# Layer norm and hi/lo split of x: the low half made by a matmul in PSUM, the norms moved to GpSimd and VectorE

## The reference, cut to what matters

```python
x = L0_attn_x                                  # (16, 512, 128) float32
xn = _layernorm(x, axis=-1)                    # (x - mean) / sqrt(var + 1e-5)
s = _L0_attn_ref(xn, ...)                      # token shift, r/k/v projections, recurrence by chunks, output projection
g = _silu(_L0_ffn_ref(xn, ...))                # gate logits = xn @ gate_W.T, top 2 of 8 experts, 8 shared experts
x = x + s * g
```

## Time and profile before

| | |
|---|---|
| median of 3 runs | 736.77 us (736.12 to 741.37) |
| the profiled execution | 736.52 us, span of its trace 734.7 us |
| busy | PE 657.6 us, DVE 575.1 us, ACT 484.7 us, POOL 454.7 us |
| granted TensorE clock, mean | 0.985 |
| `dve_choose(0)` starts | 47.51 us after the span's start |

### The profile page before, as it was taken

One profiled execution on the slowest core, in us unless ns is written; L12 is line 12 of the kernel. 1 busy time (PEld: TensorE's weight loads), 2 busy tenths in 40 slices (PEclk: granted clock), 3 DMA queues, 4 the chain that ended last, 5 costly groups with the idle time before them and its releaser, 6 DMA issues.

```text
span 734.7 us, 22308 instructions
## 1 busy us (share of the span) xinstructions
PE 657.6 (90%) x8520; PEld 457.7 (62%) x8520; DVE 575.1 (78%) x1095; ACT 484.7 (66%) x985; POOL 454.7 (62%) x490
## 2 busy tenths in 40 slices
PE   2677787997999999999999999999997899999993
PEld 1444465665666665566666667788895667666672
DVE  6989997987677886667676667666764899999996
ACT  5865578684666666566666666666665677877772
POOL 2434322225777777777777777677777566666763
PEclk9999999998999999999999999999999999999997
DMA  9931112101111232433323334323444757767642
GB/s 243 278 101 44 44 44 86 60 3 35 45 45 51 95 102 90 151 109 105 105 95 109 104 105 151 99 96 106 105 109 119 216 197 230 230 200 212 209 138 58
DMA packets 88616, 86.75 MB, mean 118 GB/s; under 512 B 11394, under 2 KB 65284, under 8 KB 88516
## 3 DMA queue, kind: packets, MB, share of 16 engines
q1 hardware_dynamic: 79428, 66.70, 29.1%
q0 software_dynamic: 9088, 18.63, 9.7%
HBM read 50.82 MB, written 34.47 MB: 116 GB/s over the span
## 4 chain that ended last, share of the span: by engine, by line
PE 43%; DVE 30%; issue 9%; POOL 8%; ACT 6%; DMA 3%; SPq 0%; DVEq 0%; ACTq 0%; POOLq 0%
PE banks L1509 7%; PE banks L1510 7%; PE banks L1511 7%; DVE wwords L1259 7%; DVE hidden L1276 6%; DVE hidden L1174 5%; PE banks L1549 5%; POOL expert_rows L629 4%; PE banks L1529 4%; PE banks L1530 4%; PE banks L1528 4%; POOL srows L619 3%; ACT hidden L747 2%; ACT hidden L743 2%; DMA srows<-normed_rows,source 2%
## 5 line engine op out<-in xcount | busy, mean ns | idle before, releaser
L747 ACT CAST hidden<-hidden 128x512 f16<-128x512 f32 x206 | 127.2, 618 | 144.1 <-DVE hidden L1174 144.0
L1178 DVE TENSOR_TENSOR hidden<-hidden 128x512 f16<-128x512 f32 x178 | 122.9, 691 | 82.4 <-ACT hidden L747 81.4
L619 POOL DMA_INDIRECT srows<-normed_rows,source x142 | 148.8, 1048 | 54.0 <-issue 40.5
L1174 DVE TENSOR_TENSOR hidden<-hidden,banks 128x512 f32<-128x512 f32 x206 | 140.7, 683 | 42.4 <-ACT hidden L743 37.1
L1528 PE MATMUL banks<-wwords,hidden 128*128 (+1 forms) x824 | 149.8, 220 | 1.4 <-DVE hidden L1178 1.0
L1530 PE MATMUL banks<-wwords,hidden 128*128 (+1 forms) x824 | 149.7, 220 | 0.0
L1529 PE MATMUL banks<-wwords,hidden 128*128 (+1 forms) x824 | 149.7, 220 | 0.0
L743 ACT ACTIVATE hidden<-banks 128x512 f32<-128x512 f32 x206 | 122.8, 596 | 27.9 <-PE banks L1511 27.7
L1509 PE MATMUL banks<-sx,wwords 128*128 128x512 f16 (+1 forms) x368 | 121.5, 330 | 0.6 <-DVE sx L1167 0.6
L1511 PE MATMUL banks<-sx,wwords 128*128 128x512 f16 (+1 forms) x368 | 121.6, 330 | 0.0
L1510 PE MATMUL banks<-sx,wwords 128*128 128x512 f16 (+1 forms) x368 | 121.5, 330 | 0.0
(11 more groups left out here) (213 smaller groups left out, 1416.0 us busy)
## 6 DMA issues: line engine op xcount, KB each, us to landing
rows<-x SPq DMA_DIRECT2D x32, 256.0 KB, 5.2
rows<-expert_rows SPq DMA_DIRECT2D x32, 256.0 KB, 3.4
normed_rows<-rows SPq DMA_DIRECT2D x16, 256.0 KB, 3.9
r_rows<-rows SPq DMA_DIRECT2D x16, 256.0 KB, 2.1
rd_rows<-rows SPq DMA_DIRECT2D x16, 256.0 KB, 2.0
stage<-r_rows SPq DMA_DIRECT2D x16, 256.0 KB, 5.4
k_rows<-rows SPq DMA_DIRECT2D x16, 256.0 KB, 2.1
kd_rows<-rows SPq DMA_DIRECT2D x16, 256.0 KB, 2.1
```

What stands on the lines that cost most here:

```text
L619: G.indirect_dma_start(srows[:, q % NXB, t, :], None, rows_in, bass.IndirectOffsetOnAxis(source[:, at:at + 1], 0)).then_inc(sem[f"s_in{q % ...
L747: A.copy(guh[:, i % 4, :], gu[:, i % 2, :]).then_inc(sem["gu_hi"], 1)
L1174: V.tensor_tensor(gu[:, i % 2, :], sg[:, i % 2, :], psum[2 * (i % 2) + 1][:, :], ALU.mult).then_inc(sem["gated"], 1)
```

## The change

- The low half: `pe_rest` adds to the transposed batch, still in its bank, the product of a negative identity and `xh` (one 128x512 float16 matmul). What is left in the bank is x minus its high half. ScalarE copies it to `xl` (`act_rest`). VectorE's `dve_flip` is gone. `minus_one` is made once by ScalarE. The transposes set the bank's start flag only with the first of four.
- The norms: ScalarE norms nothing more. VectorE norms tile 0 (`OWN_NORMS` is 1), GpSimd tiles 1 to 3, as `(row - mean) * rstd`; `shift` is gone, and the norms wait for `rstd`.
- `rates * gap` is computed by GpSimd (`pool_gaps`), ahead of its first norm.
- Order: VectorE does `dve_stats(0)` ahead of everything else. The weights' split and `dve_r_weights` follow the loop on VectorE; ScalarE's parts of the split move to its rounds 14 to 16. ScalarE copies a batch three rounds after its `std` and its rest four rounds after. On TensorE `pe_up(0)` stands behind `pe_rest(15)`.

```diff
+            def pool_gaps():
+                G.wait_ge(sem["const_in"], 16)
+                G.wait_ge(sem["rates"], 4)
+                G.tensor_tensor(wtmp[:, :, :], rep(rates[:, :], Q), rep_mid(C("gap"), HEADS), ALU.mult).then_inc(sem["gaps"], 1)
+
             def pool_norm(b):
-                G.wait_ge(sem["shift"], b + 1)
-                for t in range(b * TPS + TPS // 2, (b + 1) * TPS):
-                    G.tensor_scalar(rows[:, t, :], rows[:, t, :], rstd[:, t:t + 1], shift[:, t:t + 1],
-                                         ALU.mult, ALU.add).then_inc(sem["normed_g"], 1)
+                G.wait_ge(sem["rstd"], b + 1)
+                for t in range(b * TPS + OWN_NORMS, (b + 1) * TPS):
+                    G.tensor_scalar(rows[:, t, :], rows[:, t, :], mv[:, t, 0:1], rstd[:, t:t + 1],
+                                    ALU.subtract, ALU.mult).then_inc(sem["normed_g"], 1)
...
-            def act_norm(b):
-                A.wait_ge(sem["shift"], b + 1)
-                for t in range(b * TPS, b * TPS + TPS // 2):
-                    A.activation(rows[:, t, :], rows[:, t, :], ACT.Identity, bias=shift[:, t:t + 1],
-                                      scale=rstd[:, t:t + 1]).then_inc(sem["normed_a"], 1)
-
...
+            def act_rest(b):
+                A.wait_ge(sem["x_rest"], b + 1)
+                A.copy(xl[:, b * XS + 2:(b + 1) * XS], psum[b % 4][:, :]).then_inc(sem["x_lo"], 1)
...
-            for b in range(nb + 3):
+            for b in range(nb + 4):
                 if b < nb:
                     act_std(b)
-                if 1 <= b <= nb:
-                    act_norm(b - 1)
-                if 2 <= b < nb + 2:
-                    act_flip(b - 2)
-                if 10 <= b < 13:
-                    act_split_w(0, b - 10)
+                if 3 <= b < nb + 3:
+                    act_flip(b - 3)
+                if b >= 4:
+                    act_rest(b - 4)
+                if FIRST_SPLIT <= b < FIRST_SPLIT + 3:
+                    act_split_w(0, b - FIRST_SPLIT)
...
-                V.scalar_tensor_tensor(shift[:, T4], mv[:, T4, 0], -1.0, rstd[:, T4], ALU.mult, ALU.mult).then_inc(sem["shift"], 1)
-
-            def dve_flip(b):
-                V.wait_ge(sem["x_hi"], b + 1)
-                V.tensor_tensor(xl[:, b * XS + 2:(b + 1) * XS], psum[b % 4][:, :], xh[:, b * XS + 2:(b + 1) * XS],
-                                     ALU.subtract).then_inc(sem["x_lo"], 1)
+                for t in range(b * TPS, b * TPS + OWN_NORMS):
+                    V.tensor_scalar(rows[:, t, :], rows[:, t, :], mv[:, t, 0:1], rstd[:, t:t + 1],
+                                    ALU.subtract, ALU.mult).then_inc(sem["normed_v"], 1)
...
+            dve_stats(0)
             dve_prologue()
             dve_rates()
-            for b in range(nb + 3):
+            for b in range(1, nb + 1):
                 if b < nb:
                     dve_stats(b)
-                if 1 <= b <= nb:
-                    dve_norm(b - 1)
-                if b >= 3:
-                    dve_flip(b - 3)
-                if 11 <= b < 14:
-                    dve_split_w(0, b - 11)
-                if b >= nb + 1:
-                    dve_r_weights(b - nb - 1)
+                dve_norm(b - 1)
+            for part in range(3):
+                dve_split_w(0, part)
+            dve_r_weights(0)
+            dve_r_weights(1)
...
+            def pe_rest(b):
+                if b == 0:
+                    T.wait_ge(sem["minus_one"], 1)
+                T.wait_ge(sem["x_hi"], b + 1)
+                T.matmul(psum[b % 4][:, :], minus_one[:, :], xh[:, b * XS + 2:(b + 1) * XS], start=False, stop=True,
+                         skip_group_check=True).then_inc(sem["x_rest"], 1)
...
-            for b in range(nb + 3):
-                if 2 <= b < nb + 2:
-                    pe_flip(b - 2)
-                if b == nb + 1:
+            for b in range(nb + 2):
+                if b < nb:
+                    pe_flip(b)
+                if 1 <= b <= nb:
+                    pe_rest(b - 1)
+                if b == nb:
                     pe_up(0)
-                if b >= 3:
-                    pe_gate(b - 3)
+                if b >= 2:
+                    pe_gate(b - 2)
```

More of the change, by code:

```diff
@@ L144, in build @@
         rstd = take([P, NT])
-        shift = take([P, NT])
         gate32 = sb("gate32", [P, EXPERTS])
@@ L238, in build @@
         f2y = sb("f2y", [P, P], F16)
+        minus_one = f2
         take = carve(rows[:, :, :].rearrange("p a b -> p (a b)"))
@@ L391, in lows @@
             return sum(low_on_pool(j) == on_pool for j in range(i + 1))
+        OWN_NORMS = 1
+        FIRST_SPLIT = 14
         LOWS_FIRST = 12
@@ L463, in sp_normed @@
             def sp_normed(b):
-                nc.sync.wait_ge(sem["normed_a"], (b + 1) * TPS // 2)
-                nc.sync.wait_ge(sem["normed_g"], (b + 1) * TPS // 2)
+                nc.sync.wait_ge(sem["normed_v"], (b + 1) * OWN_NORMS)
+                nc.sync.wait_ge(sem["normed_g"], (b + 1) * (TPS - OWN_NORMS))
                 nc.sync.dma_start(rows_in[b * SEQ:(b + 1) * SEQ, :].rearrange("(t p) d -> p t d", p=P),
@@ L676, in pool_program @@
             pool_prologue()
+            pool_gaps()
             for b in range(nb):
@@ L718, in act_flip, with act_minus_one @@
                 A.copy(xh[:, b * XS + 2:(b + 1) * XS], psum[b % 4][:, :]).then_inc(sem["x_hi"], 1)
+            def act_rest(b):
+                A.wait_ge(sem["x_rest"], b + 1)
+                A.copy(xl[:, b * XS + 2:(b + 1) * XS], psum[b % 4][:, :]).then_inc(sem["x_lo"], 1)
+            def act_minus_one():
+                A.wait_ge(sem["const_in"], 16)
+                A.mul(minus_one[:, :], C("ident"), -1.0).then_inc(sem["minus_one"], 1)
             def act_split_w(k, part):
@@ L791, in act_decays @@
             def act_decays():
-                A.wait_ge(sem["const_in"], 16)
-                A.wait_ge(sem["rates"], 6)
+                A.wait_ge(sem["rates"], 5)
+                A.wait_ge(sem["gaps"], 1)
                 A.activation(wmat[:, :, :], wtmp[:, :, :], ACT.Exp, scale=-1.0).then_inc(sem["decays"], 1)
@@ L841, in act_program @@
             act_rates()
+            act_minus_one()
             act_decays()
-            for b in range(nb + 3):
+            for b in range(nb + 4):
                 if b < nb:
                     act_std(b)
-                if 1 <= b <= nb:
-                    act_norm(b - 1)
-                if 2 <= b < nb + 2:
-                    act_flip(b - 2)
-                if 10 <= b < 13:
-                    act_split_w(0, b - 10)
+                if 3 <= b < nb + 3:
[4 more added lines that the diff above has]
+                    act_split_w(0, b - FIRST_SPLIT)
             for i in range(NS + LAG):
@@ L917, in dve_rates @@
                 V.tensor_scalar(rates[:, :], rates[:, :], 200.0, None, ALU.min).then_inc(sem["rates"], 1)
-                V.wait_ge(sem["rates"], 4)
-                V.tensor_tensor(wtmp[:, :, :], rep(rates[:, :], Q), rep_mid(C("gap"), HEADS), ALU.mult).then_inc(sem["rates"], 1)
+                V.wait_ge(sem["rates"], 3)
                 V.tensor_scalar(nrate[:, :], rate[:, :], -1.0, None, ALU.mult).then_inc(sem["rates"], 1)
@@ L1419, in pe_flip @@
                     T.wait_ge(sem["const_in"], 16)
-                T.wait_ge(sem["normed_a"], (b + 1) * TPS // 2)
-                T.wait_ge(sem["normed_g"], (b + 1) * TPS // 2)
+                T.wait_ge(sem["normed_v"], (b + 1) * OWN_NORMS)
+                T.wait_ge(sem["normed_g"], (b + 1) * (TPS - OWN_NORMS))
                 for t in range(TPS):
-                    i = T.transpose(psum[b % 4][:, t * P:(t + 1) * P], rows[:, b * TPS + t, :], C("ident"))
+                    i = T.matmul(psum[b % 4][:, t * P:(t + 1) * P], rows[:, b * TPS + t, :], C("ident"), start=(t == 0), stop=(t == TPS - 1),
+                                 is_transpose=True)
                 i.then_inc(sem["flipped"], 1)
+            def pe_rest(b):
[4 more added lines that the diff above has]
+                         skip_group_check=True).then_inc(sem["x_rest"], 1)
             def pe_gate(b):
```

## The result

The changed kernel takes 749.6 us (median of 4 runs, 747.4 to 756.09) against 738.17 us for the kernel before beside it (4 runs): ratio 1.0172, interval 1.0131 to 1.0213. Run again on another occasion it took 745.68 (6 runs) against 737.66 (11 runs): 1.0125, 1.0098 to 1.0153. It is slower by 8 to 11 us; I had forecast 3.8 us faster. The profiled execution took 747.4 us, its span 745.2. The table has times in us, from that execution's trace and from the one before.

What follows compares the result with a forecast made beforehand. VectorE's own work was taken to set the prologue's pace; rounds of 1.57 us, GpSimd's norms ending at 38.2 and a 5.5 us chain put dve_choose(0) at 43.7, 3.8 sooner: 733.0 us, range 730.2 to 737.2.

Steps and rivals of the forecast that it cites:

- The head: Prologue's start: dve_stats(0) free in the wait for constants; gap product 2.3 us on GpSimd, first reciprocal at 11.8, 1.0 later.
- The round: Each prologue round falls from 2.05 to 1.57 us; the other engines hold it, GpSimd's three norms taking 1.31.
- my own list of signs: What would show the forecast right or wrong, such as GpSimd's norms above 0.45 or pe_up(0)'s matmuls 0.22 apart.
- VectorE's round: VectorE in the prologue: 2.05 less 0.60 subtraction and 0.08 shift, plus 0.20 for one norm, 1.57 us.
- The tail: Prologue's end: three splits stretch GpSimd's last norms by 1.5 us, to 38.2; then a 5.5 us chain to dve_choose(0).
- The sum: 38.2 + 5.5 puts dve_choose(0) at 43.7, 3.8 us sooner; the median time is 733.0 us.
- the part on later stages: After the prologue: what dve_choose(0) gains, the end gains, unless something late takes it back; later stages keep their length.
- My own range for the forecast: 731.8 to 734.8 us: cheap gap product and no tail contact take 2.6 off, dearer product and lost slack add 1.2.
- The higher clock: Rival, 25%: TensorE reaches its higher clock before the tail; pe_up(0) 1.3 us shorter, the rest 0.2, time 731.5.
- The rival on the slow side: Rival, 12%: TensorE and ScalarE waiting on each other set the prologue's pace, round 2.2 us, time 741.4.

Runs made afterwards that it cites:

- experiment 1: The changed kernel with GpSimd's three norms as row * rstd + shift again, shift computed by VectorE: 732.14 us against 737.14 for the kernel before, ratio 0.9938.
- experiment 2: The changed kernel with GpSimd's three tiles as (subtract mean, multiply by rstd), (multiply by rstd, add mean), (add mean, multiply by rstd); no kernel time given.
- experiment 6: The changed kernel with GpSimd's norms as (row + negated mean) * rstd, VectorE negating the means: 732.42 us against 736.75 for the kernel before, ratio 0.9924.
- experiment 10: The version of experiment 9 with ScalarE's copy of a batch two rounds after its std instead of three: 742.49 us against 736.16, ratio 1.0086.
- experiment 8: The version of experiment 7 with VectorE's three weight splits behind GpSimd's last norm and dve_r_weights ahead of them: 728.77 us against 736.75, ratio 0.9877.
- experiment 7: The version of experiment 6 with the product of rates and gaps back on VectorE: 732.22 us against 736.75 for the kernel before, ratio 0.9932.
- experiment 5: The changed kernel with two norms of a batch on VectorE and two on GpSimd: 737.58 us against 737.14 for the kernel before, ratio 1.0006.
- experiment 3: The changed kernel with GpSimd's tiles as (multiply by rstd, subtract mean), (subtract mean) alone, (subtract a constant, multiply by rstd); no kernel time given.
- experiment 4: The kernel before with GpSimd's two norms of a batch as (row - mean) * rstd: 738.68 us against 737.14, ratio 1.0033.
- experiment 9: The version of experiment 8 with the low half on VectorE again, no rest matmul and no second copy: 746.73 us against 737.66, ratio 1.0135.

## Why the prediction was wrong, by its own steps

- **The head** was right. The gap product took 1.90 us on GpSimd (2.3 taken, 1.22 to 2.47 bounded), the first reciprocal came at 11.57 (11.8). `dve_stats(0)` was free: it ran from 3.56, before the constants.
- **The round: the failed step** is the sentence that three norms on GpSimd take 1.31, 0.43 each. They took 2.32, 0.77 each. I priced the new norm by the old row and never set the two forms side by side, though the diff shows both: (multiply, add) before, (subtract, multiply) now. The operand kinds and the shape were the same, the operation was not. Experiments 1, 2 and 6 show that this alone carries the loss: with either form without a subtraction, and all else kept but for one small operation on VectorE, `dve_choose(0)` comes 10.5 to 11.4 us sooner. I had even bounded unknown prices elsewhere, but held this one for known, although my own list of signs had "GpSimd's norms longer than 0.45 in the middle of the prologue (then it sets the pace)". Why a subtraction is slow on GpSimd stays open.
- **VectorE's round.** Where GpSimd doesn't hold it, it is 1.64, not 1.57: VectorE's norm is 345 ns long and 0.26 from start to start. The 285 ns row multiplied by one scalar per partition and by a constant, the norm has two scalars per partition and a subtraction; no run tells the two differences apart. By the Trainium skill ("VectorE: DVE Perf Modes", how the mode is chosen) the norm could handle two elements a cycle, which would have made it shorter than I took it; it came out longer, and the measurement decides.
- **The tail.** Three splits beside six norms cost 1.5 us (4.17 in experiment 1, against 2.61 in experiment 10), as forecast, and experiment 8 took 1.05 of it back. The Trainium skill, "SBUF — State Buffer" (the section on its two sides), says that a VectorE operation with two SBUF inputs and a GpSimd one that reads SBUF lock each other out for whole instructions; 0.5 us lost for each 0.65 us split fits it, though no run shows that the lock lasts for the whole instruction.
- **The sum with the price mended.** Experiment 1 is close to my forecast with its assumption made true: `dve_choose(0)` at 43.87 (43.7 forecast), 732.14 us (733.0 forecast). That the numbers meet is luck: GpSimd's last norm ended at 40.11 and not at 38.2, because of the slower round, and the chain behind it took 3.76 and not 5.5, because of the higher clock. What was gained there reached the end, as the part on later stages said.
- **The range.** My own range for the forecast, 731.8 to 734.8, is not what its terms give: 2.6 off and 1.2 on make 730.4 to 734.2.
- **The rivals.** The higher clock came true in experiments 1 and 8. It was worth 1.3 us in `pe_up(0)`, as priced, and 0.6 in the transposes and the rest, where I had 0.2. The rival on the slow side had the right arithmetic and the wrong engine: it put the turning point at a round of 1.90 us, and a round of 2.32 gives 13.4 + 15 x 2.32 + 5.5 = 53.7 for the 55.2 measured. But I let only TensorE and ScalarE reach it, and gave GpSimd, which got half again as many norms, 0.2 us of slack and no rival.

## What to carry to other kernels

When an edit rewrites an operation into an algebraically equal one on GpSimd, treat it as a new operation without a price, whatever the old row says. Where work is moved to an engine, the rival to write down first is that this engine sets the pace, with the duration at which it does. Here that was 1.64 / 3 = 0.55 us a norm, and the gain was gone at 1.90 / 3 = 0.63, against an assumed 0.43. And an experiment that runs several forms side by side on tiles of one kernel settles such a price in a single run.

## What the runs showed of the hardware

- GpSimd, 128x128 float32 with scalars per partition: (multiply, add) and (add, multiply) 0.44 to 0.45 us, (subtract, multiply) 0.78 to 0.80, (multiply, subtract) 0.80, (subtract) alone 0.60, (subtract a constant, multiply) 0.72. With two tensors no such penalty shows: a subtraction of 128x512 in the feed forward part took 1.17 us (median of 28), an addition of that size 1.28. They differ in the type of the result, so this is no clean comparison. VectorE's norm was run with a subtraction only (345 ns), so what it costs there is not shown.
- In the prologue TensorE's four transposes took 1.09 us at the lower level and 0.63 at the higher. It rose between 18 and 22 us in experiments 1, 2, 6, 7 and 8, and stayed up to the last batches. With a round of 1.95 (experiment 5) it was high from 25.2 for two rounds and again at 38.9, and high in `pe_up(0)`; in experiment 3 it was high from 23.1 for three rounds. It was low throughout the rounds of the kernel before, the changed kernel and experiments 4, 9 and 10. In experiments 6 and 7 it was lost again behind a wait of 1.04 us, in experiment 2 behind one of 1.13; in experiment 1 it held through one of 1.15 us.
- The granted clock does not always tell the level: in the changed kernel it reads 1.00 from 18 to 44 us, beside transposes of 1.09, and in experiment 5 it reads 0.50 from 30 to 38 us beside the same 1.09. The lengths of the matmuls tell it.
